# Weights laid out for their products in front of an attention and ternary feed-forward kernel: rotation as a matmul, ternary values as sign times comparison

## What is computed

```python
x = x + layernorm(attention(layernorm(x)))     # 16 heads of 32, causal
x = x + layernorm(ffn(layernorm(x)))

# attention: qkv = x @ w_attn + b_attn; q and k are rotated by an angle that depends on the head
out_even = a * cos[head] - b * sin[head];  out_odd = a * sin[head] + b * cos[head]
o = softmax(q k^T, causal) * 512**-0.5 @ v;  return o @ w_proj + b_proj

# ffn: two ternary layers (512 to 2048, exact gelu, 2048 to 512)
gamma = mean(|w|);  w_hat = sign(round(w / (gamma + 1e-6))) * gamma
```

## Time and profile before

| | us |
|---|---|
| runs | 1334.47, 1337.46, 1338.87 |
| median | 1337.46 |
| the profiled execution | 1333.62 |
| its span in the profile | 1331.8 |
| busy in it: TensorE matmuls | 1192.1 (90%) |
| VectorE | 1019.6 (77%) |
| ScalarE | 769.0 (58%) |
| GpSimd | 593.6 (45%) |
| bytes moved by the queue of the kernel | 63.77 MB, 16.5% of the DMA engines' time |

### The profile page before, as it was taken

How to read it: one execution, slowest core, us unless ns; L and a number is a source line. 1 busy time by engine, 2 the same in 40 slices (tenths; PEclk the granted TensorE clock), 3 DMA queues, 4 the chain that set the end, 5 groups by cost and what they waited for, 6 DMA issues and landing times.

```text
span 1331.8 us, 24946 instructions
## 1 busy us (share of the span) xinstructions
PE 1192.1 (90%) x9364; PEld 648.4 (49%) x9364; DVE 1019.6 (77%) x2931; ACT 769.0 (58%) x1414; POOL 593.6 (45%) x636
## 2 busy tenths in 40 slices
PE   4755879999999999999999999999999999988796
PEld 2322545455545554455545554455545554554352
DVE  7588896878878797978788787968787887776532
ACT  3334874666556664666556754666466755576470
POOL 6131441692049502791159412871259313971252
PEclk9865898999999999999999999999999999999798
DMA  5451122002310113002300213002300221001000
GB/s 205 132 154 62 38 70 57 1 2 57 96 40 3 39 51 103 1 8 67 89 32 2 57 43 94 1 18 70 106 1 3 57 78 27 2 9 48 9 1 32
DMA packets 49825, 65.37 MB, mean 49 GB/s; under 512 B 8581, under 2 KB 33189, under 8 KB 49192
## 3 DMA queue, kind: packets, MB, share of 16 engines
q1 hardware_dynamic: 49704, 63.77, 16.5%
HBM read 29.89 MB, written 8.39 MB: 29 GB/s over the span
## 4 chain that ended last, share of the span: by engine, by line
PE 51%; DVE 33%; ACT 8%; POOL 3%; issue 3%; SPq 1%; DMA 1%; POOLq 0%; DVEq 0%; ACTq 0%
PE gen L488 18%; PE down L531 17%; DVE score L1089 9%; PE pv L585 4%; DVE hT L950 4%; PE score L557 4%; DVE probs L950 2%; DVE acc_add L1066 2%; PE score L563 2%; DVE mx L1089 1%; DVE qkn L1181 1%; POOL rstd L1422 1%; DVE bn L1118 1%; ACT qkn L753 1%; PE gen L548 1%
## 5 line engine op out<-in xcount | busy, mean ns | idle before, releaser
L1422 POOL TENSOR_TENSOR rstd<-veps,mhalf 128x1 f32<-128x1 f32 (+1 forms) x104 | 67.5, 649 | 472.5 <-DVE veps L1166 363.9
L809 ACT ACTIVATE probs<-score 128x512 f16<-128x512 f32 (+1 forms) x384 | 202.4, 527 | 122.1 <-PE score L557 122.1
L950 DVE TENSOR_TENSOR probs<-score,probs 128x512 f16<-128x512 f32 (+1 forms) x384 | 213.4, 597 | 61.2 <-ACT score L811 60.8
L488 PE MATMUL gen<-x2T,t1T 128*128 128x512 f16 x1024 | 242.6, 382 | 4.0 <-ACT x2T L752 2.5
L531 PE MATMUL down<-t2T,hT 128*128 128x512 f16 x1024 | 234.1, 381 | 3.5 <-DVE xn L1151 3.5
L811 ACT ACTIVATE score<-score 128x512 f32<-128x512 f32 (+1 forms) x384 | 205.4, 535 | 0.0
L488 PE MATMUL gen<-xT,wa 128*128 128x512 f16 x768 | 178.6, 383 | 12.2 <-DVE wa L970 8.4
L950 DVE TENSOR_TENSOR hT<-gen,hT 128x512 f16<-128x512 f32 x160 | 108.9, 687 | 65.8 <-ACT gen L772 27.6
L1089 DVE CUSTOM_DVE_ANT_0 score<-score,mask_rows 128x512 f32<-128x512 f32 (+1 forms) x344 | 158.0, 523 | 0.0
L531 PEld LDWEIGHTS down<-t2T,hT 128*128 128x128 f16 x1024 | 96.7, 98 | 111.3 <-DVE xn L1151 4.7
L488 PEld LDWEIGHTS gen<-x2T,t1T 128*128 128x128 f16 x1024 | 95.4, 98 | 109.4 <-ACT x2T L752 5.2
(11 more groups left out here) (136 smaller groups left out, 1838.3 us busy)
## 6 DMA issues: line engine op xcount, KB each, us to landing
qk<-qkn SPq DMA_DIRECT2D x384, 64.0 KB, 2.0
xo<-x SPq DMA_DIRECT2D x8, 1024.0 KB, 5.6
hT<-x SPq DMA_DIRECT2D x8, 1024.0 KB, 6.3
out<-xn SPq DMA_DIRECT2D x32, 256.0 KB, 2.2
hT<-w_fc SPq DMA_DIRECT2D x4, 1024.0 KB, 6.4
hT<-w_down SPq DMA_DIRECT2D x4, 1024.0 KB, 5.5
hT<-w_attn SPq DMA_DIRECT2D x4, 512.0 KB, 10.0
hT<-w_attn SPq DMA_DIRECT2D x1, 1024.0 KB, 8.7
```

The source lines that it names most:

```text
L488: mm = nc.tensor.matmul(bank[:, :], a, b, start=(start and n == 0), stop=(stop and n == len(pairs) - 1))
L809: nc.scalar.activation(probs[:, h % 2, HI, 512 * i:512 * i + n], score[i][:, 0:n], ACT.Exp, scale=1.0 / S_UP)
L950: return V.tensor_tensor(out, whole, hi, ALU.subtract)
```

## The change

The host lays the weights out differently: the query/key part of w_attn, w_fc and w_down come transposed and with each partition's data in one piece, so that the rows of the product (the contracted index) lie on the partitions. The cosine table becomes a constant matrix of 4 blocks of 128x128. On the chip:

- Rotation: `rotate(n)` is four fp32 matmuls (w as the stationary operand, the constant block as the moving one, 128 columns) into one `gen` bank, which gives the rotated weights already turned; ScalarE and VectorE evict high and low half from PSUM. There are eight. The bias is rotated by eight fp32 matmuls of one column. GpSimd's and VectorE's rotation is gone.
- Ternary weights: ScalarE writes Sign(w) as fp16 straight into `t1T` / `t2T` and then |w| in place, with its sum; VectorE replaces |w| by (|w| > theta) in place, 128x2048 at a time (`large`); GpSimd multiplies both, 16 products of 128x512 per matrix. `sign_turn`, `sign_turned` and the pairs are gone.
- Order: iteration -1 is written out on every engine. All loads are issued at once (w_qk third, then w_fc, w_v, w_proj), because w_qk, w_v and w_fc have buffers apart. Value products move to the end. All six early maxima and all of w_fc's ternary work are in iteration -1, where SP also issues w_down's loads between the `stack`s and x of batch 1. In iteration 0, `magnitudes(1, ...)` are at u = 8, 11, 15 and head 0 (`ABS_AT`), `large(1, i)` at heads 3 to 6 (`LARGE_AT`), GpSimd's products follow those. ScalarE in iteration -1: rotations 0 to 3, x of all four blocks with rotations 4 and 5 between, rotations 6 and 7, then the quarters of w_fc, each ahead of a query eviction: quarter 0, (0,0), (0,1), quarter 1, (1,0), quarter 2, (1,1), quarter 3, (2,0), value weights, (2,1), projection weights, (3,0), (3,1), values.
- `value_weights` and `projection_weights` are one instruction of 128x2048 each, where they were four of 128x512.

Its core (blank lines left out; after.py's own line numbers differ):

```diff
-FIRST_MAX = {8: 0, 11: 1}
-PAIRS = FC // 2
-PAIRS_BEFORE = PAIRS // 2
-MAGNITUDE_AT = {4: 3, 7: 0, 8: 1, 11: 2}
-PIECE_ORDER = tuple(MAGNITUDE_AT.values())
-PAIR_AT = {0: 4, 2: 5, 5: 6, 7: 7}
-PAIR2_AT = {h: PAIRS + h - 4 for h in range(4, 4 + PAIRS)}
+PIECES = EC
+ABS_AT = {8: 0, 11: 1, 15: 2}
+LARGE_AT = {3: 0, 4: 1, 5: 2, 6: 3}
...
+ROT = [("rot", n) for n in range(2 * EC)]
+XT = [("xT", tb) for tb in range(TB)]
+QK = [("qk", (g, which)) for g in range(EC) for which in range(2)]
+FIRST_USES = (ROT[0:4] + XT[0:2] + ROT[4:6] + XT[2:4] + ROT[6:8] + QK + [("v", tb) for tb in range(TB)])
...
+        t1_flat = t1T[:, :, :].rearrange("p c f -> p (c f)")
+        t2_flat = t2T[:, :, :].rearrange("p u d -> p (u d)")
+        w_qk_in = t2_flat.bitcast(f32).rearrange("p (i e) -> p i e", i=2 * EC)
+        w_stage = probs[:, :, :, :].rearrange("p b a n -> p (b a n)").bitcast(f32)
+        w_v_in = w_stage[:, 0:EC * E].rearrange("p (c n) -> p c n", c=EC)
+        rot_sb = w_stage[:, EC * E:EC * E + E].rearrange("p (g n) -> p g n", g=EC)
...
-            wa_v = w_attn.rearrange("(c p) n -> p c n", p=PARTS)
-            sp.dma_start(rope_sb.unsqueeze(1), rope.partition_broadcast(PARTS)).then_inc(rope_in, 16)
-            sp.dma_start(wa_in[:, :, 2 * E:3 * E], wa_v[:, :, 2 * E:3 * E]).then_inc(wv_in, 16)
-            for c in range(EC):
-                sp.dma_start(wa_in[:, c, 0:2 * E], wa_v[:, c, 0:2 * E]).then_inc(wqk_in[c], 16)
+            sp.dma_start(rot_sb, rot[:, :, :]).then_inc(rot_in, 16)
+            for which in range(2):
+                sp.dma_start(w_qk_in[:, EC * which:EC * (which + 1), :], w_qk[:, EC * which:EC * (which + 1), :]
+                             ).then_inc(wqk_in[which], 16)
+            sp.dma_start(b_cols[:, :], b_cols_in[:, :]).then_inc(bias_in, 16)
+            for i in range(PIECES):
+                sp.dma_start(stage[:, len_piece * i:len_piece * (i + 1)], w_fc[:, i, :]).then_inc(wfc_in[i], 16)
+            sp.dma_start(w_v_in, w_v[:, :, :]).then_inc(wv_in, 16)
+            sp.dma_start(x1[:, :, :], w_proj.rearrange("(c p) n -> p c n", p=PARTS)).then_inc(wp_in, 16)
...
+                if not here and nxt:
+                    load_x(1)
+                    stack(0)
+                    stack(1)
+                    load_down(0)
+                    stack(2)
+                    load_down(1)
+                    stack(3)
+                    load_down(2)
+                    load_down(3)
+                    return
...
+                def rotate(n):
+                    which, c = divmod(n, EC)
+                    if n == 0:
+                        pe.wait_ge(rot_in, 16)
+                    if c == 0:
+                        pe.wait_ge(wqk_in[which], 16)
+                    bank = claim("rot", n)
+                    for g in range(EC):
+                        mm = nc.tensor.matmul(bank[:, PARTS * g:PARTS * (g + 1)],
+                                              w_qk_in[:, EC * which + g, PARTS * c:PARTS * (c + 1)], rot_sb[:, g, :],
+                                              start=(g == 0), stop=True, skip_group_check=True)
+                    mm.then_inc(g_full, 1)
...
+                if nxt and not here:
+                    for n in range(4):
+                        rotate(n)
+                    pe.wait_ge(consts, CONSTS)
+                    pe.wait_ge(ident_copy, 2)
+                    x_turn(0)
+                    x_turn(1)
+                    rotate(4)
+                    rotate(5)
+                    x_turn(2)
+                    x_turn(3)
+                    rotate(6)
+                    rotate(7)
+                    bias_columns()
+                    queries_keys(0, 0)
+                    queries_keys(0, 1)
+                    queries_keys(1, 0)
+                    queries_keys(1, 1)
+                    queries_keys(2, 0)
+                    gamma_total(0)
+                    queries_keys(2, 1)
+                    max_pass(0, 1)
+                    max_pass(1, 1)
+                    max_pass(2, 1)
+                    queries_keys(3, 0)
+                    max_pass(3, 1)
+                    queries_keys(3, 1)
+                    value_bias_projected()
+                    max_pass(4, 1)
+                    values(0)
+                    max_pass(5, 1)
+                    for tb in range(1, TB):
+                        values(tb)
+                    return
...
                 def magnitudes(m, loaded, i):
                     act.wait_ge(loaded[i], 16)
-                    done = PIECES + i if m else PIECE_ORDER.index(i)
                     n = PIECES * m + i
-                    if done:
-                        act.wait_ge(g_sums, done)
-                    nc.scalar.activation(unused_out, stage[:, len_piece * i:len_piece * (i + 1)], ACT.Abs,
-                                         accum_out=gs[:, n:n + 1]).then_inc(g_sums, 1)
+                    if n:
+                        act.wait_ge(g_sums, n)
+                    flat = t2_flat if m else t1_flat
+                    cols = slice(len_piece * i, len_piece * (i + 1))
+                    nc.scalar.activation(flat[:, cols], stage[:, cols], ACT.Sign).then_inc(sign_ready, 1)
+                    act.wait_ge(sign_ready, n + 1)
+                    nc.scalar.activation(stage[:, cols], stage[:, cols], ACT.Abs, accum_out=gs[:, n:n + 1]
+                                         ).then_inc(g_sums, 1)
...
-            def rotation(c):
-                cos2 = rope_sb[:, 0:E].unsqueeze(1).to_broadcast([PARTS, 2, E])
-                dve.wait_ge(wqk_in[c], 16)
-                if c >= 2:
-                    dve.wait_ge(w_low, 1 + c - 1)
-                V.tensor_tensor(rot1[:, c % 2, :].rearrange("p (a e) -> p a e", a=2),
-                                wa_in[:, c, 0:2 * E].rearrange("p (a e) -> p a e", a=2), cos2, ALU.mult
-                                ).then_inc(rot_step, 1)
-            def rotated_low(c):
-                dve.wait_ge(wqk_hi, c + 1)
-                V.scalar_tensor_tensor(out=wa[:, LO, c, 0:2 * E], in0=rot1[:, c % 2, :], scalar=W_UP,
...
-                def ternary(pair):
-                    for k in range(2):
-                        m, u = divmod(2 * pair + k, FC)
-                        if m == 0 and k == 1:
-                            if pair:
-                                dve.wait_ge(tern_ready, 2 * pair)
-                            V.tensor_scalar(below[:, 1, :], stage[:, E * u:E * (u + 1)], theta[:, 0, 1:2], None,
-                                            ALU.is_lt).then_inc(dve_half, 1)
-                            dve.wait_ge(dve_half, pair + 1)
-                        else:
-                            dve.wait_ge(tern_half, pair + 1 if m == 0 else 2 * pair + k + 1 - PAIRS)
-                        if pair and k == 0:
-                            dve.wait_ge(sign_full, pair)
-                        V.scalar_tensor_tensor(out=t16[:, k, :], in0=stage[:, E * u:E * (u + 1)],
-                                               scalar=theta[:, m, 0:1], in1=below[:, k, :], op0=ALU.is_gt,
-                                               op1=ALU.subtract).then_inc(tern_ready, 1)
+                def large(m, i):
+                    cols = slice(len_piece * i, len_piece * (i + 1))
+                    V.tensor_scalar(stage[:, cols], stage[:, cols], theta[:, m:m + 1], None, ALU.is_gt
+                                    ).then_inc(large_ready, 1)
...
+                    magnitude(0)
+                    qk_low(2, 0)
+                    thresholds(0)
+                    large(0, 0)
+                    value_weights()
+                    qk_low(2, 1)
+                    large(0, 1)
+                    value_bias()
+                    projection_weights()
+                    large(0, 2)
+                    maxima(0, 1)
+                    maxima(1, 1)
+                    large(0, 3)
+                    maxima(2, 1)
+                    qk_low(3, 0)
+                    maxima(3, 1)
+                    qk_low(3, 1)
+                    projection_bias()
+                    maxima(4, 1)
+                    v_low(0)
+                    maxima(5, 1)
+                    for tb in range(1, TB):
+                        v_low(tb)
+                    return
                 for u in range(FC):
-                    if setup and u in PAIR_AT:
-                        ternary(PAIR_AT[u])
...
-                def under(n):
-                    m, u = divmod(n, FC)
-                    if u == 0:
-                        pool.wait_ge(g_step, 5 * m + 4)
-                    if n >= 2:
-                        pool.wait_ge(tern_ready, n - 1)
-                    P.tensor_scalar(below[:, n % 2, :], stage[:, E * u:E * (u + 1)], theta[:, m, 1:2], None,
-                                    ALU.is_lt).then_inc(tern_half, 1)
+                def ternary(n):
+                    m, b = divmod(n, FC)
+                    flat = t2_flat if m else t1_flat
```

(6 more changed lines are left out.)

376 lines of the change are left out of this document (150 added, 226 removed).

## The result

| | before | after |
|---|---|---|
| median of the runs, us | 1337.29 (1334.47 to 1338.87, 4 runs) | 1322.78 (1322.04 to 1323.69, 4 runs) |
| profiled execution, its span | 1333.62, 1331.8 | 1322.04, 1320.3 |

The ratio is 0.9891, 95% interval 0.9873 to 0.9908: 14.5 us faster by the medians, 11.6 by the two profiled executions. Forecast was 1327.4.

The account below looks back on a forecast made before the run. VectorE bounds the set-up from 76 us; the remaining 1120.9 us, TensorE 94% busy, cancel. Set-up +0.2, maxima stage -6.1 and heads -4.2 make -10.1 us: 1323.5 on the trace, 1327.4 on the median, range 1317 to 1339.

Parts of the forecast that it names:

- Rotation: Set-up: w_qk in at 9.7 us, 1.0 per rotation, ScalarE through at 24.1, query products from 25.4 instead of 43.25.
- Sign and magnitude: Set-up, w_fc on ScalarE: each quarter a Sign and an Abs, 4.1 us with the hand-over, four quarters done at 45.1.
- VectorE from 45.1: Set-up's end: `large` 1.4 us, the value and projection weight subtractions 4.9 each beside GpSimd, ending at 93.0.
- T0: Moment VectorE begins iteration 0, 92.79 us before; forecast 93.0, 0.2 later.
- Maxima stage: Iteration 0 before the first exponential: four ternary pairs leave VectorE, 1.1 and 0.8 given back; -6.1 us, bounds -7.0 and -3.
- Heads: Sixteen heads of iteration 0: 5.5 us saved by pairs leaving, 1.3 given back; -4.2 us, bounds -7 and 0.
- The 5.5 us: Saving in iteration 0's later heads from ternary pairs leaving VectorE and `sign_turn` leaving TensorE, summed as 5.5.
- Those heads stay as they are: Heads 3 to 6 of iteration 0: four `large` of 1.4 us enter as pairs leave, so no change.
- (a): Rival, set-up: GpSimd does not slow the two big subtractions; 5.2 us less, 1322.2; chance 0.22.
- (b): Rival: GpSimd slows `large` too, to twice 1.4; six of eight cost 8.4 us, 1335.8; chance 0.15.
- (c): Rival, set-up: products after 45 us stay at 1.2 GHz; 15.7 us more, values 1 to 3 8.0 of it, 1343.1; chance 0.10.
- (d): Rival: second sixteen GpSimd products end after the heads, so `o_turned(0)` waits and ternary work is only late; given no chance.

Follow-up runs that it names:

- fill_heads: Changed kernel plus five needless matmuls of 384 columns behind each head from 4 on; 1321.45 us, ratio 0.9883.
- before_tiny: Kernel before, with VectorE's sixteen halves for w_down 32 columns wide instead of 512; 1329.68 us, one run.
- pool_after: Changed kernel with GpSimd's products of each matrix begun only after its fourth `large`; 1319.92 us, ratio 0.9867.
- before_tiny_noturn: Kernel before, with w_down's halves 32 columns wide and `sign_turn` of those pairs one transposition instead of eight; 1334.52 us, one run.
- the reordered kernel: Changed kernel with iteration -1 in another order, 1310.20 us; the 0.81 is with GpSimd's products also behind each matrix's fourth comparison, 1309.31 us.
- pool_narrow: Changed kernel with GpSimd's products cut from 128x512 to 128x128, four times as many; 1323.23 us, one run.

## Why the prediction was right, and where it was not

**Rotation: right.** w_qk's half landed at 9.37 (9.7), a rotation took 1.1 and 1.0 (2.20 and 2.05 for two), 1.35 in the first four; ScalarE was through at 23.96 (24.1), query products started at 24.97 (25.4).

```profile
9.37 5.40 PE L607 MATMUL gen<-probs,t2T 128*128 128x128 f32 x32 [9.37 <-DMA t2T<-w_qk]
...
24.97 13.11 PE L468 MATMUL gen<-xT,wa 128*128 128x512 f16 x60
43.93 0.59 PE L439 MATMUL down<-gt,ones 128*128 128x1 f32 x2 [5.85 <-DVE gt L1023]
44.38 5.28 PE L468 MATMUL gen<-xT,wa 128*128 128x512 f16 x12
```

**Sign and magnitude: right, 1.5 us too long.** A quarter took 3.8, since the reading of the sum overlaps; Sign is 1.90 like Abs. TensorE idled 5.85 us (6.4), then started slow: 5.28 for the twelve behind `gamma_total`, and 4.79 for group (3,0), where I had 4.5.

**VectorE from 45.1: the failed step.** "By the 1024-element rows, 1.21 against 2.45, they take 4.9 each" is false: 2.3, 5.2 us less on the chain. Against that `large` was 1.29, then 2.14 and 2.18 instead of 1.4, and the copy 1.12 instead of 0.17: 2.2 more in all. With ScalarE's 1.5 that makes 4.5 of the 5.0 us by which T0 was early (in fill_heads, with the same set-up, T0 was 1.5 us earlier still). The rest of the chain ran as worked out: query group (3,1) 2.76 (2.7), the value bias 3.62 (3.6), three value products 7.93 (8.1).

**Maxima stage: 1.4 us too small.** VectorE's busy time fell by 7.0 and its other time in the stage by 0.5. The 1.1 us of bank waits and the 0.8 of longer quarters that I gave back did not show. The third quarter did end late, 0.2 us read included, and released the first exponential with no idle time between them:

```profile
119.93 0.19 ACT L860 ACTIVATION_READ_ACCUMULATOR hT<-hT 128x1 f32 x1
120.02 0.58 ACT L817 ACTIVATE probs<-score 128x512 f16<-128x512 f32 x1
```

**Heads: wrong in sign, the second failed step.** The 5.5 us doesn't follow from its own terms: two of 1.0, two of 1.3, 0.9 and 0.4 make 5.9 (4.6 if the 1.3 is for both together); and 2.0 less 0.87 is 1.1, not 1.3. As a size it was too large: narrowing all eight pairs by 7.5 us of VectorE's work gave 3.9 (before_tiny). "Those heads stay as they are" for `large` in place of a pair left out GpSimd: 1.5 (pool_after). The longer quarter was no cost of 1.3: head 1 has 0.95 more, head 2 0.85 less. And nothing in the sum said that taking `sign_turn` off TensorE could have a price. In the kernel before it was 1.0 in one profile (before_tiny_noturn), little more than the scatter; in the reordered kernel the heads ran at 0.81, and filler gave 4.4 us back. If the 1.0 is taken as it stands, 3.9 less 1.5 and 1.0 leaves 1.4 gained where 1.3 was lost; the 2.7 between is `large` itself and what the order of waits adds, and was not separated. So the failed size is shown, and the cause of the loss only in part.

**Rivals.** (a) gave 1322.2 and its mechanism held: the subtractions were not slowed, though by the order of arrival, not for want of contention. That its time fits the median of 1322.8 is chance, as it took the forecast's heads. (b) was half there: five of eight `large` grew, by one wait of 0.9 and not to twice. (c) did not happen in this profile; in pool_narrow, behind a wait of 5.23 us, the value products ran partly at 1.2 GHz and took 1.25 us more, not the 8.0 that (c) had for them. (d) did not happen.

**The scale.** On the trace's clock I had 1323.5 and it was 1322.04. I added 3.8 us, as the median before lay above its profiled execution; after, it lies 0.7 above. That is 3.1 of the 4.6 us between forecast and result.

## What to carry to other kernels

When an engine's instruction is long beside another engine, ask whether it was slower or waited: lay its end against the other's last end, and see whether the excess follows its own length or the other's. If it waited, let the other engine go last. Cutting that engine's instructions short makes most waits short too, but an unbroken run of short ones can hold the waiting engine for its whole length: here 5.5 us for an instruction of 0.43. And when work leaves TensorE in a stage where it often waits, price the clock: the removed transpositions may have been what kept the remaining products at full speed. Before reading a stage from one profile, look how far it lies apart in two kernels that share its instructions.

## What was not expected of the hardware

VectorE and GpSimd exclude each other by the instruction: excess of 0.1 to 0.2, 0.9 and up to 1.9 us on a comparison of 1.28 beside products of 0.43, 1.16 and 2.13 us. But a scaling of 0.43 us took 5.98 beside a run of 0.43 us products. The 512-column maxima and the low halves of queries and keys, which read PSUM, kept 0.69 and 0.75 us beside GpSimd. Needless matmuls made a stage 4.4 us shorter, because the granted clock went from 0.81 to 0.96.
